# SyncE asks for weight pieces 3 to 9 once the piece two ahead has landed

## The reference

```
h = relu(layernorm(x))
q = h @ wq.T + bq ; k = h @ wk.T + bk ; v = h @ wv.T + bv
q2 = q @ wiq.T + biq ; k2 = k @ wik.T + bik ; v2 = v @ wiv.T + biv
mask[src, dst] = softplus(edge_type_weights)[edge_type - 1]      # -inf without an edge
x = x + (softmax(q2 k2^T / 8 + mask) v2) @ wo.T + bo             # per head of width 64
h = relu(layernorm(x))
u = h @ root + bias + sum over r of mean_of_neighbours_r(h) @ weight[r]      # 8 relations
z = concat(u, h) @ w_gate + b_gate
out = x + tanh(u) * z + h * (1 - z)
```

## Time and profile before

| | us |
|---|---|
| median of 3 runs | 227.75 (226.43 to 230.03) |
| the profiled execution, its own time | 226.06 |
| its span, first to last instruction | 224.3 |
| TensorE busy | 214.3 (96% of the span) |
| VectorE, GpSimd, ScalarE busy | 85.1, 25.5, 21.4 |
| mean DMA rate over the span | 343 GB/s |
| granted TensorE clock | full in the whole span |

### The profile page before, as it was taken

The page is one execution under the profiler, slowest core; times in us unless marked ns, Lnnn a source line. Parts: engine busy times, 40 slices in busy tenths (PEclk is TensorE's granted clock), DMA queues, the critical chain, the costliest instruction groups (busy, mean ns, idle before and its releaser), DMA issues.

```text
span 224.3 us, 10195 instructions
## 1 busy us (share of the span) xinstructions
PE 214.3 (96%) x4789; PEld 208.5 (93%) x4789; DVE 85.1 (38%) x150; ACT 21.4 (10%) x41; POOL 25.5 (11%) x57
## 2 busy tenths in 40 slices
PE   2999989999999998999999999999999999989993
PEld 2899989999999998799999999999999999989993
DVE  2469847231699721458978500000000000000624
ACT  2432000000110120311224000000000000000101
POOL 3365006400000000010000950000000000000000
PEclk9999999999999999999999999999999999999999
DMA  6999999999999999999999999999999999994002
GB/s 217 393 382 425 424 418 394 396 321 370 359 380 378 375 348 381 396 384 412 387 348 367 384 394 359 361 340 386 402 352 380 337 367 368 361 419 188 3 3 70
DMA packets 14697, 77.02 MB, mean 343 GB/s; under 512 B 4880, under 2 KB 5152, under 8 KB 5440
## 3 DMA queue, kind: packets, MB, share of 16 engines
q1 hardware_dynamic: 14112, 75.96, 88.3%
q10 hardware_dynamic: 544, 0.42, 0.6%
HBM read 75.97 MB, written 0.39 MB: 340 GB/s over the span
## 4 chain that ended last, share of the span: by engine, by line
PE 95%; DMA 1%; issue 1%; DVE 1%; ACT 0%
PE acc L796 82%; PE acc L1040 4%; DMA x_sb<-in_x 1%; PE turn L983 1%; PE side L844 1%; PE side L983 1%; PE side L1040 1%; PE turn L872 1%; DVE stats L513 1%; PE acc L814 1%; PE turn L884 0%; PE side L855 0%; PE turn L855 0%; PE acc L884 0%; PE side L837 0%
## 5 line engine op out<-in xcount | busy, mean ns | idle before, releaser
L796 PE MATMUL acc<-mean,raw 128*64 128x96 f32 x2048 | 85.1, 246 | 0.7 <-issue 0.7
L796 PEld LDWEIGHTS acc<-mean,raw 128*64 128x64 f32 x2048 | 84.8, 137 | 0.9 <-issue 0.9
L796 PE MATMUL acc<-hT,raw 128*64 128x96 f32 x1024 | 44.7, 247 | 1.4 <-issue 1.3
L796 PEld LDWEIGHTS acc<-hT,raw 128*64 128x64 f32 x1024 | 43.0, 137 | 2.7 <-issue 2.4
L759 DVE TENSOR_TENSOR uT<-acc,uT 128x384 f32<-128x384 f32 x2 | 1.1, 558 | 82.3 <-PE acc L796 82.3
L796 PE MATMUL acc<-qT,raw 128*64 128x96 f32 x512 | 22.0, 247 | 0.0
L796 PEld LDWEIGHTS acc<-qT,raw 128*64 128x64 f32 x512 | 21.4, 137 | 0.4 <-issue 0.3
L796 PE MATMUL acc<-kT,raw 128*64 128x96 f32 x512 | 21.7, 246 | 0.0
L796 PEld LDWEIGHTS acc<-kT,raw 128*64 128x64 f32 x512 | 21.3, 137 | 0.3 <-issue 0.3
L796 PE MATMUL acc<-uT,raw 128*64 128x96 f32 x256 | 11.9, 258 | 0.0
L796 PEld LDWEIGHTS acc<-uT,raw 128*64 128x64 f32 x256 | 11.5, 146 | 0.3 <-ACT uT L415 0.2
(11 more groups left out here) (178 smaller groups left out, 148.0 us busy)
## 6 DMA issues: line engine op xcount, KB each, us to landing
raw<-in_weights SPq DMA_DIRECT2D x284, 256.0 KB, 4.8
raw<-in_weights SPq DMA_DIRECT2D x1, 1024.0 KB, 6.1
x_sb<-in_x SPq DMA_DIRECT2D x1, 192.0 KB, 3.3
x_sb<-in_x ACTq DMA_DIRECT2D x1, 192.0 KB, 3.8
out<-out_rows SPq DMA_DIRECT2D x1, 192.0 KB, 2.1
out<-out_rows ACTq DMA_DIRECT2D x1, 144.0 KB, 2.5
out<-out_rows SPq DMA_DIRECT2D x1, 48.0 KB, 2.2
bias_rows<-in_biases ACTq DMA_DIRECT2D x1, 36.0 KB
```

The source lines that it names most:

```text
L796: mm = pe.matmul(a[g * HD:(g + 1) * HD, b, c * N:(c + 1) * N], raw[:, s, at:at + HD], moving(k0 + k), start=opens and k0 == 0 and c == 0 a ...
```

## The change

In `fetch`, pieces 3 to 9 get a wait of their own: SyncE issues piece n only when piece n - 2 has landed in full. Nothing else is altered: neither the order of the pieces, nor their sizes and slots, nor any engine but SyncE. Pieces 0, 1 and 2 are issued without a wait, as before, and pieces from 10 on wait for their slot, as before.

```
                 if n >= SLOTS:
                     sp.wait_ge(piece_used, n - SLOTS + 1)
+                elif n >= 3:
+
+                    sp.wait_ge(raw_landed[n - 2], landed(n - 2))
                 for part in transfers(n):
                     sp.dma_start(raw[part, n % SLOTS, :], weights[where, part]).then_inc(raw_landed[n % SLOTS], 16)
```

## The result

The changed kernel takes 230.37 us (median of 6 runs, 229.05 to 232.26) against 228.05 us before (6 runs, 225.59 to 230.03). The ratio is 1.0143, with a 95% interval of 1.0096 to 1.0189: slower by 1.4%, or some 3 us. The ratio is taken from the fast runs alone, of both kernels, so it isn't that of the two medians, which are 2.3 us or 1.0% apart. The profiled execution took 229.15 us, 3.1 us more than the one before.

What follows compares the result with a forecast made beforehand. The prediction took TensorE's own program to bound the kernel: 226.06 us profiled + 0 for SyncE's waits + 0 behind = 226.1; the runs' median lies 1.7 higher, so 227.8 us, range 226.2 to 230.6.

Steps and rivals of the forecast that it cites:

- rival (a): Shallow queue runs partly dry in pieces 3 to 9: L stays 4.8 us, price 2.1, some 229.9 us; chance 0.19.
- What bounds the kernel: From 7 to 45 us TensorE's own program sets the time; weights are always there, with no stall on `raw`.
- slack: How long before its use a piece has landed: 1.3 us at piece 3, 1.9 at 7, 4.3 at 10.
- The thresholds: Values of L above which TensorE waits for pieces 3 to 10; lowest 4.1 us, at piece 7.
- L: Time from the issue of a piece's last part to its landing; taken as 3.6 us, plausible 3.1 to 4.8.
- How large is L: Estimate for pieces 3 to 9: 3.6 us, the middle of x's halves, 192 KB each, at 3.3 and 3.8.
- What comes behind: From piece 10, issued 3.4 us late, the queue refills some 0.3 us per piece and cover grows; cost 0.
- the formula: For pieces 3 to 9, landing(n) = landing(n - 2) + 1.95 + L; piece 10 lands at 9.9 + 3 x (1.95 + L) + 4.5 + L.
- (b): Latency isn't queue at all: L stays 6.7 us, piece 9 is 9.2 us late, 237.0 us; chance 0.07.
- (c): A little faster: waits for weights and the 0.7 us "issue" stall at 28.5 us may go, 226.4 us; chance 0.08.
- (d): The waits do nothing because pieces land before SyncE gets there; forecast time unchanged; chance 0.66 together with no cost.
- Other engines: ScalarE's small transfers may land earlier while SyncE is silent from 6.8 to 9.9 us; that gains nothing.

Runs made afterwards that it cites:

- e8: The kernel before the change, run again with no edit: 227.46 us, ratio 1.0020.
- e4: The kernel before, with the same seven two-ahead landing waits placed on pieces 43 to 49 in place of 3 to 9: 226.40 us, ratio 0.9958.
- e9: The kernel before, with pieces 43 to 46 each waiting for the piece directly ahead to land: 231.65 us, ratio 1.0205 to the kernel before.
- e6: The changed kernel with its seven waits, every piece sent as one 1 MB transfer: 236.31 us, ratio 1.0406 to the kernel before.
- e12: The changed kernel with two-ahead waits on pieces 3, 4 and 5 alone: 227.49 us, ratio 1.0128 to the kernel before.
- e2: The changed kernel with pieces 4 to 9 waiting for the piece three ahead: 225.65 us, ratio 0.9969 to the kernel before.
- e7: The kernel before, without landing waits, every piece sent as one 1 MB transfer: 237.21 us, ratio 1.0431.
- e11: The changed kernel with a three-ahead landing wait on every piece from 4 on: 224.68 us, ratio 0.9891 to the kernel before.
- e10: The changed kernel's limit counted in parts, part j of piece n waiting for part j of piece n - 2: 226.95 us, ratio 1.0004 to the kernel before.
- e5: The changed kernel with the two-ahead landing wait on every piece from 3 on: 259.26 us, ratio 1.1462 to the kernel before.
- e1: The changed kernel run again with no edit: 229.51 us, ratio 1.0187 to the kernel before.
- e3: The changed kernel with only piece 3 waiting for a landing: 227.69 us, ratio 1.0031 to the kernel before.

## Why the prediction was wrong

The forecast was 227.8 us and no cost; the measured time is 230.37, inside the range of 226.2 to 230.6, and the change costs 1.4%, clear of noise. It is rival (a), to which I gave 0.19 and 229.9 us.

**What bounds the kernel: right.** TensorE's program sets the time, no weights were waited for (e8 again), and the slack is thinnest at pieces 3 to 7. e4 shows what the slack is worth.

**The thresholds: right.** "4.1 us is the point from which the change costs", with piece 7 first. L came out at a mean of 4.4, and TensorE's first wait was for piece 7.

**How large is L: here it failed.** I took 3.6 from the halves of x (3.3 and 3.8 us) and shut off larger values by the argument that with L at 5.0 the engines would be idle for 2 of 7 us, "and then there is no queue that could make L 5.0". Measured were 4.4 and 5.3 (means in two profiles), a pair in 6.5 to 7.7 us, and a DMA busy share of 0.89 and 0.87: the engines idled some tenth of the time, less than 2 of 7 us, and needed longer for each byte. Of the 3.3 us by which piece 7 landed later than my 26.6, 2.8 are L (13.6 us for pieces 3, 5 and 7 in place of 10.8) and 0.4 SyncE's issues, one of which took 1.44 us. The argument took for granted that L above the bound is queueing. e9 took the queue away and L was still 3.9 to 5.4, so most of it isn't queue. Its shares of start, data and counting of the landing weren't measured, but e6 shows some 2 us between nearly the last data and the landing. The rows of x were 192 KB on engines with nothing yet ahead of them, and even their upper end, 3.8, was below every value but one in the changed kernel.

**What comes behind: failed too.** I had "the landings stay bound by the data rate" and slack that grows from piece 10 on. TensorE's two longest waits were there: piece 10 was asked for at 33.1, not 29.2, its L was 5.9, and the rate stayed at 311 GB/s until 40 us. With L = 4.4 in the formula, piece 10 lands at 37.9; it landed at 40.9. e12's piece 6 shows the same after-effect. The formula had one L for all pieces, and L was largest in those behind the waits.

**The rivals.** (a) was right in mechanism and near in size, with waits at pieces 7, 10 and 12 where it had 7 and 9. (b), latency that isn't queue at all, is half right: the queue's share of the 6.7 us is 1.3 to 2.8 us (6.7 less e9's 5.4 and 3.9), not all and not none. The Trainium skill's rule ("DMA: Bandwidth & Descriptors", rules for kernel authors: issue early, wait late) agrees with the runs: two pieces don't cover the fixed cost, three do (e2). That page's fit of 2.0 us plus bytes at 436 GB/s (section on the anatomy of a DMA), for GpSimd's queue, would give an estimate of 2.6 us for a part; alone, from SyncE's queue, it took 3.9 to 5.4 (e9). (c) had a grain of truth: fewer "issue" stalls came (0.7 us against 2.0), far less than the waits cost. The stall of 0.7 us near 29 us, of which (c) spoke, is in all profiles whose first ten pieces have no landing wait (before, e4, e7, e8; 0.4 us in e9) and in none that has one. (d) was excluded rightly: SyncE did wait until 10.07 us.

**Other engines: right.** No new wait on their operands came.

**What stays open.** Why the engines are busy longer per byte after a hole, and for how long; why part of a landing's time stays when nothing is ahead; most of e11's gain; and how much of the cost the first three waits bring (e12). Of the 3.7 us by which piece 12 was late, the runs separate the grain of the limit (e10), its depth (e2) and its place (e4), but not the shares of holes and slower bytes.

## What to carry to other kernels

A limit on transfers under way is a rate: window over round trip (2.1 MB in 6.9 us, 305 GB/s, in e5), where the round trip counts issue, start, data and the counting of the landing. Measure the round trip with one transfer alone under the kernel's load before taking it from a row at the kernel's start, and let the window refill in small steps rather than when a whole piece is in. Such a limit costs only where a slack is thin, so compare it with the slack piece by piece, behind the limit as well as in it; and too deep a queue can cost as well, as whole pieces showed (e6, e7).

## What the runs showed that I had not expected

- With many whole pieces queued TensorE itself stops: 8.9 us of "issue" stalls in 15 places with up to ten 1 MB transfers queued (e7), against 0.3 to 2.6 us in all kernels with four parts per piece at full clock. In e6, whole pieces too, there is no such stall while two pieces at most are under way; the first comes at 41 us, where e7's come from 29 us on. That speaks for the depth and not the size, but no run changes one alone. That they are instruction loads behind weights in the same engines is likely (the page counts 37 packets, 0.61 MB, on the instruction queue) but no run took those loads apart; e10, with 2.6 us in 5 stalls, doesn't fit a plain rule by depth.
- SyncE needs 0.59 us for a part of 256 KB, and this pace is a useful limit by itself: issuing whole pieces in 0.33 us each (e6) frees SyncE, and the kernel with them is 4% slower (e7).
- Piece 0 took from 3.7 to 5.4 us in these profiles with the same code, beside 2.8 for a later piece; the granted clock was 1.00 over it in the shortest and the longest alike. Where SyncE is silent from 6.8 us until piece 1 has landed it took 4.6 to 5.4 us (the changed kernel, e1, e3, e5, e12), in the others with four parts 3.8 to 4.6. Whether the silence lengthens it isn't shown. In the changed kernel piece 1 so began at 13.22 us, not 12.11; that doesn't add to the delay of piece 12, which hung on landings alone.
